# Thirty of 64 gathered rows fetched by TensorE instead of 28, with a uniform pairing of batches

## The chip, the cores and the metric

The kernel runs on one core of a Trainium2 chip. The metric is the device time of one execution in microseconds (us). Shares and rows are from one execution taken by the hardware profiler.

## The reference, cut to what matters

An image batch `x` (32 images, 64 channels, 16x16 pixels) goes through a group norm and a 3x3 convolution, a graph attention over 80,000 edges, and a mixture-of-experts block whose gate is a graph attention over 262,144 edges. The change touches only that last gate:

```
h = (x_flat @ W_gat).reshape(M, 4, 4)          # M = 8192 tokens
a_src = (h * att_src).sum(-1);  a_dst = (h * att_dst).sum(-1)
e     = leaky_relu(a_src[src] + a_dst[dst], 0.2)
ee    = exp(e - segment_max(e, dst)[dst]);  denom = segment_sum(ee, dst)
agg   = segment_sum(h[src] * (ee / denom[dst])[:, :, None], dst) + b_gat
```

So each edge needs the 16 numbers `h[src]` of its source node and the 4 numbers `a_src[src]`.

## The kernel before, in words

The edges lie sorted by destination, 128 partitions times 64 edges to a *chunk*. In this data 17 chunks hold edges (numbers 0 to 16). For chunks 0 and 1 GpSimd (POOL) fetches all 64 rows of `h` per partition from memory, one indirect DMA for each of the 64 columns (`g_gather`, L845). From chunk 2 on, 15 chunks in all, it fetches only 36 columns and the other 28 (`PICKS`, L65) are *picked* on chip: TensorE multiplies one-hot columns with `h_split`, a three-part bf16 copy of the table.

The 28 columns go in 7 batches of 4 (`BATCH`, `BATCHES`), and two batches share one set of one-hots (a *pair*, `w`; pair 3 has one batch and is 512 columns wide, the others 1024). The steps for chunk c are:

- `pick_keys` (L1965, VectorE): eight small operations turn the source numbers into keys; once for a chunk.
- `spread(m)` (L1061, TensorE): 4 matmuls lay the keys of batch m along the free axis of a PSUM bank.
- `all_keys(m)` (L1296, ScalarE): casts that bank into `pick_all`.
- `one_hot(w)` (L1990, VectorE): 8 comparisons (one for each of 8 table slices) write `pick_hot[w % 2]`.
- `pick(m)` (L1071, TensorE): 96 matmuls (4 columns x 8 slices x 3 parts) into one of two PSUM banks. It waits for the pair's one-hots and for batch m-2 to be taken (`pick_taken`).
- `take_picked(m)` (L1998, VectorE): a product from PSUM (L2002, recorded at L1391) and a reduce (L2006); the product's end releases `pick_taken`.
- `picked_a_src` (L2008, VectorE): `a_src` of the picked rows.

While chunk c is picked, the softmax work of chunk c-1, the chunk behind, is done between the takes: `flags`, then `edge_scores`, `maximum`, `messages`, `weighted_sums` on VectorE (L1922 to L1958), and `lay`, `weigh`, `rows` on ScalarE (L1259 to L1294). `lay` waits until all gathers of chunk c-1 have landed (L1270), and `edge_scores` waits for `lay`; `messages` waits for `weigh`; `rows` waits for `weighted_sums` (L1290) and copies the sums out. POOL may gather chunk c+1 once `messages` of chunk c-1 is done (`g_used`, L861). SyncE reloads index buffers after `lay` (L713).

Each engine runs its instructions in the order in which they stand in the code; nothing reorders them. The orders in the loop before are, for chunk c ((c+1) marks steps for the next chunk):

```
VectorE  flags | oh1 take0 edge_scores | take1 maximum | oh2 take2 messages |
         take3 weighted_sums | oh3 take4 | keys(c+1) take5 | oh0(c+1) take6 | a_src
TensorE  p0 s4 p1 s5 p2 s6 p3 p4 p5 s0(c+1) s1(c+1) p6 s2(c+1) s3(c+1)
ScalarE  lay k4 k5 weigh k6 rows k0(c+1) k1(c+1) k2(c+1) k3(c+1)
```

Here p is `pick`, s `spread`, k `all_keys`, oh `one_hot`.

Of the kernel before, what the change touches and what calls it, by code (L numbers as in the profile page):

```python
# [61 lines left out]
HID = 2 * CH  # L62


PICKS = 28  # L65
BATCH = 4
BATCHES = PICKS // BATCH
HOTS = -(-BATCHES // 2)
CANDS = 8
K_TILES = NT // CANDS  # L70
YT_FREE = 24
# [170 lines left out]
def build(nc, io, debug=None):  # L242
    with ExitStack() as ctx:
# [319 lines left out]
        def bc(ap, shape):  # L563
            return ap.to_broadcast(shape)

        def chunk_count(it, b, per, n):

            return it * (2 * per) + ((b - 2) * per + n)

        def turn_of(b, m):  # L570

            return (b * BATCHES + m) % 2

        def hot_of(w):

            return min(2, BATCHES - 2 * w) * BATCH * P


        @block.sync
# [291 lines left out]
        def _(pe):  # L871
# [189 lines left out]
            def spread(it, b, m):  # L1061

                if m == 0:
                    pe.wait_ge(pick_keys_set, it * 2 + (b - 1))
                pe.wait_ge(pick_all_set, chunk_count(it, b, BATCHES, m + 1))
                for k in range(BATCH):
                    last = nc.tensor.matmul(ps[turn_of(b, m)][:, k * P:(k + 1) * P], bc(pick_key[b][:, BATCH * m + k:BATCH * m + k + 1], [P, P]), ident16,  # L1067
                                            start=True, stop=True)
                last.then_inc(pick_spread, 1)

            def pick(it, b, m):  # L1071
                pe.wait_ge(pick_hot_set, chunk_count(it, b, HOTS, m // 2 + 3))
                pe.wait_ge(pick_taken, chunk_count(it, b, BATCHES, m + 1))
                for k in range(BATCH):
                    for t in range(K_TILES):
                        for n in range(SPLITS):
                            last = nc.tensor.matmul(ps[2 + turn_of(b, m)][:, k * PICK_W:(k + 1) * PICK_W], pick_hot[m // 2 % 2][t][:, (m % 2 * BATCH + k) * P:(m % 2 * BATCH + k + 1) * P],  # L1077
                                                    h_split[n][:, t * PICK_W:(t + 1) * PICK_W],
                                                    start=t == 0 and n == 0, stop=t == K_TILES - 1 and n == SPLITS - 1)
                last.then_inc(picked, 1)  # L1080
# [1 line left out]
            pe.wait_ge(h_split_set, 2)  # L1082
            pe.wait_ge(g_count_set, 1)

            pe.sem_inc(picked, 2)
            n_all = pe.value_load(g_count[0:1, 0:1], min_val=2, max_val=G_CHUNKS)
            with pe.If(n_all >= 3):
                for m in range(4):
# [1 line left out]
            with nc.Fori(1, G_CHUNKS // 2, engines=[mybir.EngineType.PE], hint_back_edge=True) as it:  # L1090
                for b in range(2):
                    with pe.If(it * 2 + b < n_all):
                        for m in range(BATCHES - 2):
                            pick(it, b, m)
                            if m + 4 < BATCHES:
                                spread(it, b, m + 4)
                        for m in range(2):
                            pick(it, b, BATCHES - 2 + m)
                            with pe.If(it * 2 + (b + 1) < n_all):
                                for k in range(2):  # L1100
                                    spread(it + b, 1 - b, 2 * m + k)


            pe.wait_ge(exp_taken, EXPERTS_EARLY)
# [56 lines left out]
        def _(act):  # L1161
# [59 lines left out]
            def weigh(c):  # L1221
                act.wait_ge(a_scored, c + 1)
                nc.scalar.activation(a_weight, a_score, ACT.Exp)
                nc.scalar.activation(a_msg[:, CH * A_RUN:], a_score, ACT.Exp).then_inc(a_weighed, 1)
# [71 lines left out]
            def all_keys(it, b, m):  # L1296
                act.wait_ge(pick_spread, chunk_count(it, b, BATCHES, m + 1))
                act.wait_ge(pick_hot_set, chunk_count(it, b, HOTS, m // 2 + 1))
                nc.scalar.copy(pick_all[m // 2 % 2][:, m % 2 * BATCH * P:(m % 2 + 1) * BATCH * P], ps[turn_of(b, m)][:, 0:BATCH * P]).then_inc(pick_all_set, 1)  # L1299

            def gelu(n):
                act.wait_ge(hid_done, n + 1)
# [17 lines left out]
            with act.Fori(1, G_CHUNKS // 2 + 1) as it:  # L1320
                for b in range(2):
                    with act.If(it * 2 + b < n_all):
                        lay(it, 1 - b, 1)
                        all_keys(it, b, 4)
                        all_keys(it, b, 5)
                        weigh(it, 1 - b, 1)
                        all_keys(it, b, 6)
                        rows(it, 1 - b, 1)
                        with act.If(it * 2 + (b + 1) < n_all):
                            for m in range(4):  # L1330
                                all_keys(it + b, 1 - b, m)
                    with act.If(it * 2 + b == n_all):
                        lay(it, 1 - b, 1)
                        weigh(it, 1 - b, 1)
                        rows(it, 1 - b, 1)
# [36 lines left out]
        def _(dve):  # L1372
# [17 lines left out]
            def tt(o, a_, b_, op):  # L1390
                return V.tensor_tensor(o, a_, b_, op)  # L1391
# [568 lines left out]
            def pick_link(it, b, ins):  # L1960
                p_done[0] += 1
                ins.then_inc(dve_pick, 1)
                dve.wait_ge(dve_pick, chunk_count(it, b, PICK_STEPS, p_done[0]))
# [25 lines left out]

            def one_hot(it, b, w):  # L1990

                dve.wait_ge(pick_all_set, chunk_count(it, b, BATCHES, min(2 * w + 2, BATCHES) + 2))
                dve.wait_ge(picked, chunk_count(it, b, BATCHES, (1, 2, 4, 6)[w]))
                for t in range(K_TILES):
                    ins = ts(pick_hot[w % 2][t][:, 0:hot_of(w)], pick_all[w % 2][:, 0:hot_of(w)], node[:, t:t + 1], ALU.is_equal)
                ins.then_inc(pick_hot_set, 1)

            def take_picked(it, b, m):  # L1998
                dve.wait_ge(picked, chunk_count(it, b, BATCHES, m + 3))
                at = slice(m * BATCH, (m + 1) * BATCH)  # L2000
                prod_ = pick_prod.rearrange("p (j k f) -> p j k f", k=CANDS, f=G_HF)
                pick_link(it, b, tt(prod_, ps[2 + turn_of(b, m)][:, 0:BATCH * PICK_W].rearrange("p (j k f) -> p j k f", k=CANDS, f=G_HF),  # L2002
                                    bc(pick_of[b].rearrange("p (j k) -> p j k", k=CANDS)[:, at, :, None], [P, BATCH, CANDS, G_HF]), ALU.mult))
                dve.sem_inc(pick_taken, 1)  # L2004
                lo = G_RUN - PICKS + m * BATCH
                pick_link(it, b, V.tensor_reduce(hs[b][:, lo:lo + BATCH, 0:G_HF], prod_.rearrange("p j k f -> p j f k"), AX_X, ALU.add))  # L2006

            def picked_a_src(it, b):  # L2008
                rows_ = hs[b][:, G_RUN - PICKS:]
# [19 lines left out]
            with nc.Fori(1, G_CHUNKS // 2 + 1, engines=[mybir.EngineType.DVE], head_slot={mybir.EngineType.DVE: 0}) as it:  # L2029
                for b in range(2):  # L2030
                    with dve.If(it * 2 + b < n_all):
                        p_done[0] = 0
                        flags(it, 1 - b, 1)
                        for m in range(BATCHES - 2):
                            if m % 2 == 0:
                                one_hot(it, b, m // 2 + 1)
                            take_picked(it, b, m)
                            if m < 4:
                                (edge_scores, maximum, messages, weighted_sums)[m](it, 1 - b, 1)
                        for m in range(2):  # L2040
                            dve.sem_inc(waits_carried, 1)
                            with dve.If(it * 2 + (b + 1) < n_all):
                                if m == 0:
                                    pick_keys(it + b, 1 - b)
                                    dve.sem_inc(waits_carried, 1)
                                else:
                                    one_hot(it + b, 1 - b, 0)
                            take_picked(it, b, BATCHES - 2 + m)
                        picked_a_src(it, b)
                        dve.sem_inc(waits_carried, 1)  # L2050
                        assert p_done[0] == PICK_STEPS
                    with dve.If(it * 2 + b == n_all):
                        flags(it, 1 - b, 1)
                        edge_scores(it, 1 - b, 1)
                        maximum(it, 1 - b, 1)
                        messages(it, 1 - b, 1)
                        weighted_sums(it, 1 - b, 1)
                        V.tensor_copy(row_tail, g_didx[1 - b][:, G_RUN - 1:G_RUN])
                        dve.sem_inc(waits_carried, 1)
# [178 lines left out]
```

## Time and profile before

| what | us |
|---|---|
| median of 3 runs (lowest, highest) | 2579.01 (2577.95, 2585.97) |
| the profiled execution's own time | 2578.7 |
| its span, first to last instruction | 2576.9 |
| busy: VectorE / GpSimd / TensorE matmul / ScalarE | 1802.0 / 1751.2 / 1149.8 / 681.6 |

```profile
## 2 busy tenths in 40 slices
PE   4552000001011000100105497789888898798286
DVE  8888679997879989884327301168768777778356
ACT  1110004434445343534201011222222222222121
POOL 0005777777777777777778577777777777777470
PEclk9775555555555555555555555589999999999558
```

Each digit is the busy share, in tenths, of one fortieth of the span, 64.4 us. The gate's chunk loop fills slices 27 to 37. A POOL that issues DMAs back to back reads 7, because the time between two issues is not counted as busy.

### The profile page before, as it was taken

What the parts mean: (1) busy time and instruction counts of PE and PEld (TensorE: products, weight loads), DVE (VectorE), ACT (ScalarE), POOL (GpSimd) and SP (SyncE); (2) the same over time, 40 slices, a digit from 0 to 9 for tenths busy, and PEclk for the clock granted to TensorE, in tenths of its full rate; (3) what the DMA queues carried; (4) which work ended last, traced back from release to release, by engine and by line L of the source; (5) the groups of instructions that cost most, each with busy time, mean ns of one, the idle gap of its engine ahead of it and who ended that gap; (6) DMA issues with size and microseconds to landing.
All of it is one profiled execution on the core that took longest, in us unless ns stands there. A gap on an engine that the chain in (4) does not pass through costs nothing.

```text
span 2576.9 us, 33597 instructions
## 1 busy us (share of the span) xinstructions
PE 1149.8 (45%) x12439; PEld 966.3 (37%) x12439; DVE 1802.0 (70%) x2767; ACT 681.6 (26%) x696; POOL 1751.2 (68%) x1690
## 2 busy tenths in 40 slices
PE   4552000001011000100105497789888898798286
PEld 2221000001000000000004254489888898798266
DVE  8888679997879989884327301168768777778356
ACT  1110004434445343534201011222222222222121
POOL 0005777777777777777778577777777777777470
PEclk9775555555555555555555555589999999999558
DMA  9402113333323333334314416122222222221101
GB/s 350 178 1 71 49 62 104 103 100 99 99 84 101 100 102 100 100 100 134 99 32 44 78 45 155 23 26 30 38 26 29 38 27 28 38 29 22 31 10 34
DMA packets 138177, 187.94 MB, mean 73 GB/s; under 512 B 77628, under 2 KB 96254, under 8 KB 131438
## 3 DMA queue, kind: packets, MB, share of 16 engines
q1 hardware_dynamic: 83958, 122.34, 14.6%
q0 software_dynamic: 54080, 63.61, 14.3%
q8 instruction: 105, 1.72, 0.3%
q14 instruction: 34, 0.28, 0.0%
HBM read 98.53 MB, written 87.32 MB: 72 GB/s over the span
## 4 chain that ended last, share of the span: by engine, by line
POOL 63%; issue 21%; DVE 10%; PE 3%; DMA 1%; ACT 1%; POOLq 0%; DVEq 0%; SPq 0%; ACTq 0%
POOL arena L751 59%; DVE arena L1391 8%; POOL d_adseed L841 2%; POOL d_qseed L775 2%; PE psum L1124 1%; PE psum L1155 1%; PE psum L1038 1%; DVE arena L1394 1%; DMA arena<-in_x 1%; PE psum L1050 1%; DMA arena<-d_gdst,arena 0%; PE psum L874 0%; ACT arena L1194 0%; DVE arena L1403 0%; PE psum L1116 0%
## 5 line engine op out<-in xcount | busy, mean ns | idle before, releaser
L1391 DVE TENSOR_TENSOR arena<-arena 128x512 f32<-128x512 f32 (+17 forms) x1331 | 766.3, 615 | 218.0 <-DMA arena<-d_ac,arena 65.7
L751 POOL DMA_INDIRECT arena<-d_h,arena x668 | 675.8, 1012 | 203.6 <-issue 203.6
L751 POOL DMA_INDIRECT arena<-in_kv,arena x640 | 662.3, 1035 | 195.0 <-issue 195.0
L1077 PE MATMUL psum<-arena 128*128 128x128 bf16 x10080 | 598.4, 222 | 45.1 <-DVEq L2004 29.8
L1077 PEld LDWEIGHTS psum<-arena 128*128 128x128 bf16 x10080 | 587.0, 99 | 50.1 <-DVE arena L1394 19.3
L874 PE MATMUL psum<-arena 128*128 128x128 f32 (+3 forms) x402 | 92.2, 399 | 1041.6 <-DVEq L1467 803.4
L874 PEld LDWEIGHTS psum<-arena 128*128 128x128 f32 (+3 forms) x402 | 70.5, 206 | 1064.3 <-DVEq L1467 818.5
L1391 DVE TENSOR_TENSOR arena<-psum,arena 128x512 f32<-128x512 f32 (+2 forms) x179 | 142.2, 802 | 231.3 <-PE psum L1038 202.6
L1394 DVE TENSOR_SCALAR arena<-arena 128x1024 bf16<-128x1024 f16 (+10 forms) x707 | 256.4, 414 | 35.1 <-DVE arena L2006 11.0
L751 POOL DMA_INDIRECT arena<-d_adst,arena x40 | 54.5, 1362 | 220.3 <-DVEq L1638 208.4
L1038 PEld LDWEIGHTS psum<-arena 128*128 128x128 f32 x512 | 113.7, 328 | 146.7 <-issue 110.4
L1038 PE MATMUL psum<-arena 128*128 128x64 f32 x512 | 125.1, 427 | 54.8 <-ACT arena L1305 38.5
L1792 DVE TENSOR_TENSOR_SCAN psum<-psum,arena 128x1024 f32<-128x1024 f32 x40 | 91.9, 2298 | 79.7 <-ACT arena L1218 78.5
L1050 PE MATMUL psum<-arena 64*128 64x512 f32 x128 | 131.5, 1135 | 0.6 <-ACT arena L1343 0.6
L1214 ACT COPY arena<-arena 128x1984 f32<-128x1984 f32 x20 | 73.1, 3655 | 214.6 <-DMA arena<-d_qseed 147.2
L1232 ACT COPY arena<-arena 128x2304 f32<-128x2304 f32 x20 | 87.8, 4391 | 155.5 <-DVEq L1814 155.5
L2006 DVE TENSOR_REDUCE arena<-arena 128x64 f32<-128x512 f32 x105 | 106.3, 1012 | 16.9 <-DVE arena L1391 11.5
L1305 ACT ACTIVATE arena<-psum,arena 128x512 f32<-128x512 f32 x64 | 43.7, 687 | 222.7 <-PE psum L1050 222.6
L1293 ACT COPY arena<-arena 128x1280 f32<-128x1280 f32 x17 | 57.3, 3373 | 158.7 <-DVEq L1957 158.7
L751 POOL DMA_INDIRECT arena<-d_gs,arena x64 | 67.2, 1050 | 42.6 <-SPq L734 23.4
L1391 DVE TENSOR_TENSOR arena<-arena,psum 128x2048 f32<-128x2048 f32 (+4 forms) x47 | 88.5, 1882 | 6.6 <-ACT psum L1285 2.3
L1299 ACT CAST arena<-psum 128x512 f16<-128x512 f32 x105 | 57.3, 587 | 133.4 <-PE psum L1067 133.4
(189 smaller groups left out, 1479.8 us busy)
## 6 DMA issues: line engine op xcount, KB each, us to landing
d_gs<-arena SPq DMA_DIRECT2D x32, 768.0 KB, 13.5
d_as<-arena SPq DMA_DIRECT2D x20, 1152.0 KB, 4.4
d_qseed<-arena SPq DMA_DIRECT2D x5, 4096.0 KB, 31.4
arena<-d_qseed SPq DMA_DIRECT2D x20, 1024.0 KB, 5.1
arena<-d_h,arena POOLq DMA_INDIRECT x668
arena<-in_kv,arena POOLq DMA_INDIRECT x640
d_adseed<-arena SPq DMA_DIRECT2D x1, 4096.0 KB, 29.2
arena<-in_w_blocks SPq DMA_DIRECT2D x1, 2304.0 KB, 20.2
```

The lines of the kernel that those rows point to most:

```text
L751: return pool.indirect_dma_start(out, None, table, bass.IndirectOffsetOnAxis(index[:, t:t + 1], 0))
L874: return nc.tensor.transpose(out, in_, ident[0:n, 0:n])
L1038: last = nc.tensor.matmul(ps[6 + k // 2][:, k % 2 * 256 + e * CH:k % 2 * 256 + (e + 1) * CH], hid[n % 2][:, k * P:(k + 1) * P], w2[:, e, : ...
L1050: nc.tensor.matmul(ps[4 + n % 2][:, :], w1[at, e, :], yT[at, i0:i0 + 4, :].rearrange("p i n -> p (i n)"), start=True, stop=True).then_inc( ...
L1077: last = nc.tensor.matmul(ps[2 + turn_of(b, m)][:, k * PICK_W:(k + 1) * PICK_W], pick_hot[m // 2 % 2][t][:, (m % 2 * BATCH + k) * P:(m % 2 ...
L1214: nc.scalar.copy(by_f[:, :, 1:], q_seed[b].rearrange("p j f -> p f j")[:, :, 1:])
L1232: nc.scalar.copy(a_rows[b].rearrange("p j f -> p f j"), a_sum.rearrange("p (f j) -> p f j", j=A_RUN)).then_inc(a_rows_set, 1)
L1293: nc.scalar.copy(rows_f[:, 0:G_F], g_sum.rearrange("p (f j) -> p f j", j=G_COLS)[:, :, 1:])
L1391: return V.tensor_tensor(o, a_, b_, op)
L1394: return V.tensor_scalar(o, a_, s1, s2, op0, op1) if op1 is not None else V.tensor_scalar(o, a_, s1, None, op0)
L1792: step(V.tensor_tensor_scan(q_edge, a_go, q_fm[:, at], 0.0, ALU.mult, ALU.add))
L2006: pick_link(it, b, V.tensor_reduce(hs[b][:, lo:lo + BATCH, 0:G_HF], prod_.rearrange("p j k f -> p j f k"), AX_X, ALU.add))
```

## The change

`PICKS` goes from 28 to 30, so POOL gathers 34 columns of each chunk from chunk 2 on. The batches become 8: seven of 4 columns and a last of 2. They form four pairs; the last pair is 768 columns wide. The waits are rewritten for this. Three orders change: the softmax work of the chunk behind starts after take1 instead of take0; the next keys are made before one-hot 3; the next chunk's first one-hots come after take5 and before take6 and take7.

```
VectorE  flags | oh1 take0 | take1 edge_scores | oh2 take2 maximum | take3 messages |
         keys(c+1) oh3 take4 weighted_sums | take5 | oh0(c+1) take6 take7 | a_src
TensorE  p0 s4 p1 s5 p2 s6 p3 s7 p4 p5 s0(c+1) s1(c+1) p6 s2(c+1) s3(c+1) p7
ScalarE  k4 lay k5 k6 weigh k7 rows k0(c+1) k1(c+1) k2(c+1) k3(c+1)
```

```diff
-PICKS = 28
+PICKS = 30
-BATCHES = PICKS // BATCH
-HOTS = -(-BATCHES // 2)
+BATCHES = -(-PICKS // BATCH)
+HOTS = BATCHES // 2
...
+        PICKED_FIRST = 4
+        def batch_of(m):
+            return min(BATCH, PICKS - m * BATCH)
         def hot_of(w):
-            return min(2, BATCHES - 2 * w) * BATCH * P
+            return (batch_of(2 * w) + batch_of(2 * w + 1)) * P
...
                         for m in range(2):
-                            pick(it, b, BATCHES - 2 + m)
                             with pe.If(it * 2 + (b + 1) < n_all):
                                 for k in range(2):
                                     spread(it + b, 1 - b, 2 * m + k)
+                            pick(it, b, BATCHES - 2 + m)
...
                     with act.If(it * 2 + b < n_all):
+                        all_keys(it, b, 4)
                         lay(it, 1 - b, 1)
-                        all_keys(it, b, 4)
                         all_keys(it, b, 5)
+                        all_keys(it, b, 6)
                         weigh(it, 1 - b, 1)
-                        all_keys(it, b, 6)
+                        all_keys(it, b, 7)
                         rows(it, 1 - b, 1)
                         with act.If(it * 2 + (b + 1) < n_all):
                             for m in range(4):
...
             def one_hot(it, b, w):
-                dve.wait_ge(pick_all_set, chunk_count(it, b, BATCHES, min(2 * w + 2, BATCHES) + 2))
-                dve.wait_ge(picked, chunk_count(it, b, BATCHES, (1, 2, 4, 6)[w]))
+                dve.wait_ge(pick_all_set, chunk_count(it, b, BATCHES, 2 * w + 4))
+                dve.wait_ge(picked, chunk_count(it, b, BATCHES, 2 * w + PICKED_FIRST - 2))
...
                         for m in range(BATCHES - 2):
+                            if m == 4:
+                                dve.sem_inc(waits_carried, 1)
+                                with dve.If(it * 2 + (b + 1) < n_all):
+                                    pick_keys(it + b, 1 - b)
+                                    dve.sem_inc(waits_carried, 1)
                             if m % 2 == 0:
                                 one_hot(it, b, m // 2 + 1)
                             take_picked(it, b, m)
-                            if m < 4:
-                                (edge_scores, maximum, messages, weighted_sums)[m](it, 1 - b, 1)
+                            if 1 <= m <= 4:
+                                (edge_scores, maximum, messages, weighted_sums)[m - 1](it, 1 - b, 1)
+                        dve.sem_inc(waits_carried, 1)
+                        with dve.If(it * 2 + (b + 1) < n_all):
+                            one_hot(it + b, 1 - b, 0)
                         for m in range(2):
-                            dve.sem_inc(waits_carried, 1)
-                            with dve.If(it * 2 + (b + 1) < n_all):
-                                if m == 0:
-                                    pick_keys(it + b, 1 - b)
-                                    dve.sem_inc(waits_carried, 1)
-                                else:
-                                    one_hot(it + b, 1 - b, 0)
                             take_picked(it, b, BATCHES - 2 + m)
                         picked_a_src(it, b)
```

`spread`, `pick`, `all_keys` and `take_picked` loop over `batch_of(m)` columns instead of `BATCH`. The first count given to `picked` goes from 2 to `PICKED_FIRST`.

## Rows read from the trace of the kernel before

**Rows 1.** The page: part 4 (chain by engine), part 5 (the gathers of `d_h`)
```profile
POOL 63%; issue 21%; DVE 10%; PE 3%; DMA 1%; ACT 1%; POOLq 0%; DVEq 0%; SPq 0%; ACTq 0%
...
L751 POOL DMA_INDIRECT arena<-d_h,arena x668 | 675.8, 1012 | 203.6 <-issue 203.6
```

**Rows 2.** Timeline (start us, us, engine, line, op), ScalarE: `lay`'s last copy
```profile
1788.22 0.20 ACT L1272 COPY arena<-arena 128x4 f32<-128x4 f32 x1 [5.62 <-DMA arena<-d_h,arena]
...
2407.93 0.20 ACT L1272 COPY arena<-arena 128x4 f32<-128x4 f32 x1 [11.27 <-DMA arena<-d_h,arena]
```

**Rows 3.** Timeline, VectorE, chunk 3: a chunk in which it hardly waits
```profile
1738.20 0.43 DVE L1391 TENSOR_TENSOR arena<-arena 128x256 f32<-128x256 int32 x1 [0.61 <-DVE arena L2012]
...
1742.09 0.68 DVE L1391 TENSOR_TENSOR arena<-psum,arena 128x512 f32<-128x512 f32 x1
...
1745.96 0.69 DVE L1391 TENSOR_TENSOR arena<-psum,arena 128x512 f32<-128x512 f32 x1
...
1747.85 0.70 DVE L1941 TENSOR_TENSOR_SCAN arena<-arena 128x260 f32<-128x260 f32 x1
...
1750.14 3.26 DVE L1394 TENSOR_SCALAR arena<-arena 128x1024 bf16<-128x1024 f16 x8 [0.31 <-DVE arena L1391]
...
1755.20 2.29 DVE L1391 TENSOR_TENSOR arena<-arena,psum 128x1024 f32<-128x1024 f32 x1
...
1759.54 2.87 DVE L1956 TENSOR_TENSOR_SCAN arena<-psum,arena 128x1300 f32<-128x1300 f32 x1
1762.70 2.54 DVE L1394 TENSOR_SCALAR arena<-arena 128x512 bf16<-128x512 f16 x8 [0.30 <-DVE arena L1956]
...
1767.41 0.42 DVE L1394 TENSOR_SCALAR arena<-arena 128x28 int32<-128x28 int32 x2 [0.42 <-DVE arena L2006]
...
1769.89 0.69 DVE L1391 TENSOR_TENSOR arena<-psum,arena 128x512 f32<-128x512 f32 x1
...
1772.16 3.49 DVE L1394 TENSOR_SCALAR arena<-arena 128x1024 bf16<-128x1024 f16 x8 [0.41 <-DVE arena L2006]
1775.57 0.68 DVE L1391 TENSOR_TENSOR arena<-psum,arena 128x512 f32<-128x512 f32 x1
1776.39 1.01 DVE L2006 TENSOR_REDUCE arena<-arena 128x64 f32<-128x512 f32 x1
1777.43 0.63 DVE L1391 TENSOR_TENSOR arena<-arena 128x448 f32<-128x448 f32 x1
...
1779.70 0.42 DVE L1391 TENSOR_TENSOR arena<-arena 128x256 f32<-128x256 int32 x1 [0.99 <-DVE arena L2012]
```

**Rows 4.** Timeline, ScalarE, chunk 3: `rows` (two copies), then two casts of `all_keys`
```profile
1762.49 3.38 ACT L1293 COPY arena<-arena 128x1280 f32<-128x1280 f32 x1 [9.86 <-DVEq L1957]
1765.60 0.92 ACT L1294 COPY arena<-arena 128x256 f32<-128x256 f32 x1
1769.12 1.07 ACT L1299 CAST arena<-psum 128x512 f16<-128x512 f32 x2 [2.60 <-PE psum L1067]
```

**Rows 5.** Timeline, TensorE: picks at full clock, with one `spread` between and without
```profile
1745.22 0.39 PE L1067 MATMUL psum<-arena 128*128 128x128 f16 x4
1745.44 5.52 PE L1077 MATMUL psum<-arena 128*128 128x128 bf16 x96
...
1751.03 16.24 PE L1077 MATMUL psum<-arena 128*128 128x128 bf16 x288
```

**Rows 6.** Timeline, TensorE: after a wait for `pick_keys`, at the lower clock
```profile
1908.55 1.03 PE L1067 MATMUL psum<-arena 128*128 128x128 f16 x8 [3.17 <-DVEq L1982]
1909.37 7.90 PE L1077 MATMUL psum<-arena 128*128 128x128 bf16 x96
```

**Rows 7.** Timeline, VectorE: take1 of chunk 2, then the softmax work of chunk 16
```profile
1705.00 0.69 DVE L1391 TENSOR_TENSOR arena<-psum,arena 128x512 f32<-128x512 f32 x1 [1.81 <-PE psum L1077]
...
2408.16 0.70 DVE L1932 TENSOR_TENSOR_SCAN arena<-arena 128x260 f32<-128x260 f32 x1 [13.61 <-ACT arena L1272]
...
2414.36 2.28 DVE L1391 TENSOR_TENSOR arena<-arena,psum 128x1024 f32<-128x1024 f32 x1 [2.31 <-ACT psum L1285]
```

More of the change, by code:

```diff
@@ L1065, in spread @@
                 pe.wait_ge(pick_all_set, chunk_count(it, b, BATCHES, m + 1))
-                for k in range(BATCH):
+                for k in range(batch_of(m)):
                     last = nc.tensor.matmul(ps[turn_of(b, m)][:, k * P:(k + 1) * P], bc(pick_key[b][:, BATCH * m + k:BATCH * m + k + 1], [P, P]), ident16,
@@ L1073, in pick @@
                 pe.wait_ge(pick_taken, chunk_count(it, b, BATCHES, m + 1))
-                for k in range(BATCH):
+                for k in range(batch_of(m)):
                     for t in range(K_TILES):
@@ L1083, in _ @@
             pe.wait_ge(g_count_set, 1)
-            pe.sem_inc(picked, 2)
+            pe.sem_inc(picked, PICKED_FIRST)
             n_all = pe.value_load(g_count[0:1, 0:1], min_val=2, max_val=G_CHUNKS)
@@ L1298, in all_keys @@
                 act.wait_ge(pick_hot_set, chunk_count(it, b, HOTS, m // 2 + 1))
-                nc.scalar.copy(pick_all[m // 2 % 2][:, m % 2 * BATCH * P:(m % 2 + 1) * BATCH * P], ps[turn_of(b, m)][:, 0:BATCH * P]).then_inc(pick_all_set, 1)
+                nc.scalar.copy(pick_all[m // 2 % 2][:, m % 2 * BATCH * P:(m % 2 * BATCH + batch_of(m)) * P], ps[turn_of(b, m)][:, 0:batch_of(m) * P]).then_inc(pick_all_set, 1)
             def gelu(n):
@@ L1998, in take_picked @@
             def take_picked(it, b, m):
[L1999 to L2003, printed above, removed]
+                dve.wait_ge(picked, chunk_count(it, b, BATCHES, m + 1 + PICKED_FIRST))
+                n_ = batch_of(m)
+                at = slice(m * BATCH, m * BATCH + n_)
+                prod_ = pick_prod[:, 0:n_ * PICK_W].rearrange("p (j k f) -> p j k f", k=CANDS, f=G_HF)
+                pick_link(it, b, tt(prod_, ps[2 + turn_of(b, m)][:, 0:n_ * PICK_W].rearrange("p (j k f) -> p j k f", k=CANDS, f=G_HF),
+                                    bc(pick_of[b].rearrange("p (j k) -> p j k", k=CANDS)[:, at, :, None], [P, n_, CANDS, G_HF]), ALU.mult))
                 dve.sem_inc(pick_taken, 1)
                 lo = G_RUN - PICKS + m * BATCH
-                pick_link(it, b, V.tensor_reduce(hs[b][:, lo:lo + BATCH, 0:G_HF], prod_.rearrange("p j k f -> p j f k"), AX_X, ALU.add))
+                pick_link(it, b, V.tensor_reduce(hs[b][:, lo:lo + n_, 0:G_HF], prod_.rearrange("p j k f -> p j f k"), AX_X, ALU.add))
             def picked_a_src(it, b):
```

## The prediction

> **What bounds the kernel now.** I read the chain of waits first, then the largest group on it, then one chunk on each engine. The chain lies on POOL for 63% of the span, and all idle time before the gathers of `d_h` is "issue": POOL never waits for another engine there [rows 1]. One gather costs (675.8 + 203.6) / 668 = 1.316 us, so 36 should take 47.4. The period shows it: `lay`'s last copy, which waits for the landing of a chunk's gathers, starts at 1788.22 for chunk 3 and at 2407.93 for chunk 16, 13 periods of 47.67 us [rows 2]. The reader is to see that ScalarE was idle there "until DMA". VectorE follows: in its pass for chunk 3, where it waits for almost nothing, it needs 1779.70 - 1738.20 = 41.5 us [rows 3]. At the end it waits 13.61 us for the last gathers, and from 2408.16 on the tail begins [rows 7]. The change doesn't touch the tail, so the question is only when that row starts.
>
> **What the change removes.** Two gathers in each of 15 chunks, 30 x 1.316 = 39.5 us of POOL. If POOL stayed the bound, the period would be 47.67 - 2.63 = 45.0 and the tail would start 39.5 us earlier, at 2368.7.
>
> **What it adds on VectorE.** Batch 7 has two columns. A full take is 1777.43 - 1775.57 = 1.86 us (product 0.68, reduce 1.01) [rows 3]; half the columns I put at 1.2 (bounds 0.9 and 1.86). One-hot 3 grows from 512 to 768 columns: before, it and take4 take 1767.41 - 0.42 - 1762.70 = 4.3, so one-hot 3 is 2.4; a full one is 3.3; between them 2.8. Together +1.6: 43.1 us of VectorE, under 45.0. The keys and `a_src` of 30 columns instead of 28 are below 0.1.
>
> **What it adds on TensorE.** A pick with one spread is 5.59 (1751.03 - 1745.44), a pick without one (16.24 - 5.52) / 2 = 5.36, so a column's picks are 1.34 and its spread 0.06 [rows 5]: 30 columns are 42 us at the full clock. That too is under 45.0.
>
> **What the new order does: the step that decides.** Sums of busy time are not the period. ScalarE's order is ... `rows`, then `all_keys` 0 and 1 of the next chunk. Before, `weighted_sums` followed take3; `rows` ran from 1762.49 to 1766.52 beside one-hot 3 and take4, and the casts came at 1769.12, after the keys [rows 4]. Now `weighted_sums` follows take4, and only take5 stands between it and the next one-hots, which need both casts. `rows` takes 4.03, the casts 1.07, with 0.1 at each end: 5.3 us from the end of `weighted_sums`. Take5 hides 1.9 of them; VectorE stands for 3.3. TensorE stands too: s2 waits for the first cast, and p7 is queued behind it. Making the keys early doesn't help, as the spreads they feed find ScalarE occupied.
>
> The longest loop through the engines, from the start of take1:
> - take1 1.89 (1747.85 - 1745.96); `edge_scores` 2.0 (1745.96 - 1742.09 - 1.86) and 0.2 before the next; one-hot 2 and take2 5.06 (1755.20 - 1750.14); `maximum` 2.29 - 0.31 = 1.98 [rows 3]. At 11.1. Pick 3 is ready then as well (two picks of 5.59 after pick 1).
> - `messages` needs `weigh`, 2.31 after `maximum` [rows 7]. Before, a one-hot and a take hid that; now take3 alone does, so 0.4 shows. At 13.4.
> - `messages` 2.45; keys 2.48 and some 0.3 before them; one-hot 3 2.8; take4 1.88; `weighted_sums` 2.87 [rows 3]. At 26.2.
> - `rows` and casts 5.3, at 31.5; one-hot 0 3.3 (3.49 busy, next op 3.41 later), at 34.8: take6 starts.
> - take6's product releases p0 0.9 later; p0 5.59, p1 5.56: take1 of the next chunk at 46.8. By VectorE alone (take6 1.86, take7 1.2, `a_src` and the gap 2.3, flags and one-hot 1 3.89, take0 1.86) it would be 45.9, so TensorE closes the loop.
>
> That is 46.8 at the full clock. On TensorE p6 ends at 27.9 and s2 comes at 30.9: a gap of 3.0 in each chunk, then two spreads half a microsecond apart, then p7. Before, eleven passes (chunks 5 to 15) had a wait of 3.2 for the keys. After four of them the spreads and pick 5 ran as in [rows 6], 1.03 and 7.90 against 0.6 and 5.52, a loss of 2.8; after two more the loss was 1.3; after five nothing. Here p7 ends 1.3 before p0 could start, so the long loss costs 1.5 and the short none: 4/11 x 1.5 = 0.55 a chunk. I take 47.4; bounds 46.8 (never) and 48.7 (every time, 1.9).
>
> The Trainium skill, page "TensorE: Matmul & The Clock Gate", section "HAM oscillation — how this bites in real kernels", says that a matmul loop with a wait in every pass can be thrown back to the low clock in every pass. By that rule the sum goes by the upper bound; the rows above agree only after some of the waits.
>
> **Waits and queues with no price.** `lay` moves behind `all_keys` 4, so it starts only after p0 and s4, about 2 us into the pass; `edge_scores` now comes after take1, 7 us in, and covers that. SyncE's index loads hang on `lay`; the next keys use them 15 us later. `all_keys` 5 is queued behind `lay`, so late gathers would hold s7 and one-hot 2; with VectorE behind POOL this doesn't bite. `messages` comes later, and POOL waits for it before chunk c+1; POOL has a whole chunk's gathers (45 us) to issue meanwhile, and by my period it runs ahead by 2.4 a chunk, some 34 us in all, about when that wait begins to hold it, harmlessly.
>
> **The sum.** Take1 of chunk 2 is at 1705.00 [rows 7], and all before it is unchanged. Its take6: 1739.8. Take6 of chunk 15: 13 periods on. The pass of chunk 16 has no keys and no next one-hots: take1 comes 12.0 after that, take6 waits for p6 at 12.0 + 27.9 = 39.9, take7 for p7 at 42.7; then take7 1.2, `a_src` and gap 2.3, flags 0.8: `edge_scores` of chunk 16 at 47.0. So it starts at 1786.8 + 13 x period. With 47.4 that is 2403.0, against 2408.16: 5.2 earlier. POOL is done by then (2368). The profiled execution took 2578.7 (1.8 of it around the span, 0.3 below the median of the runs); less 5.2 this gives 2573.5.
>
> **Forecast: 2573 us** (rounded down), 0.2% under the median, within the 0.3% (7.7 us) that a measurement can tell from no change. Its own range, from periods of 46.9 to 48.2, is 2567 to 2584. What is late next is ScalarE: VectorE's wait for gathers turns into a wait for its casts.
>
> **Rivals.**
> - *POOL stays the bound.* Then `rows` must not hold the casts, or VectorE must make up 2.4 a chunk elsewhere. For: 43.1 and 42 are both under 45.0. Against: ScalarE's queue order is in the code, and nothing in it overtakes. 2578.7 - 39.5 = 2539, or up to 2545 if the gathers that ran long beside one-hots stay as many. It would need a period under 44.8 by my formula. 13%.
> - *The clock never falls.* TensorE is busy for 42 of 47 us instead of 39 of 47.7, and has one gap of 3.0 instead of several. Period 46.8, start 2395.2, so 2565.7. 15%.
> - *The clock falls in every chunk: slower.* Place: the gap from p6 to s2, lengthened by two spreads that are hardly work. Price: 1.9 on p7 and p0, 48.7; start 2419.9, 11.7 later, 2590.4. It decides from a period of 47.8 on, where 1786.8 + 13 x period passes 2408. For: a gap that lies in front of near-idle time. Against: five of eleven such waits before cost nothing. 19%.
>
> The forecast has 53%: its spread crosses the lower bound, so 20 of the 53 count as faster, 30 as the same, 3 as slower. POOL and the full clock are faster (13, 15); the fallen clock gives 4 same and 15 slower. Faster 0.48, same 0.34, slower 0.18. The range reaches from 2550 to 2591; outside are POOL's 13% and about 6% above.
>
> **What would show it.** Right: the casts of `all_keys` 0 and 1 start directly behind `rows` with no idle time; one-hot 0 has about 3 us of idle time, released by ScalarE L1299; the spreads s2 wait for ScalarE; the flags-to-flags period is 47 to 48; POOL's last gathers of `d_h` have landed near 2368, long before the softmax work of chunk 16, which no longer waits for it. The first row in which `messages` waits for ScalarE L1285 has some 0.4 idle. Wrong: `lay` still waits for DMA at a period of 45, or POOL waits for VectorE from early on, or the wait for the casts is under 1 us.

## The result, and the profile after

The changed kernel takes 2570.12 us (median of 6 runs, 2565.67 to 2572.32) against 2578.48 for the kernel before (2577.45 to 2585.97): ratio 0.9961, 95% interval [0.9947, 0.9976]. Timed again in another job it was 2569.83 against 2576.92, ratio 0.9973 [0.9963, 0.9983]. The forecast was 2573 and an unmeasurable gain; the gain is small, 7 to 8 us, but it is clear of noise: both intervals end below 1. Most of the 39.5 us that POOL was relieved of did not arrive, as forecast.

The profiled execution took 2572.32, with a span of 2570.5. The page of the changed kernel, parts 4 and 5, and the loop's list of waits (engine, line, waited for: us, times, longest) answer to [rows 1]:

```profile
POOL 40%; DVE 23%; issue 17%; PE 15%; ACT 3%; DMA 1%; DVEq 1%; POOLq 0%; ACTq 0%; SPq 0%
...
L757 POOL DMA_INDIRECT arena<-d_h,arena x638 | 643.6, 1009 | 205.1 <-issue 196.3 <-DVEq L1960 8.2 <-DMA arena<-d_gdrow 0.6
```

```profile
DVE arena L1401 <- ACT arena L1305: 40.0, 13, 3.1
...
POOL arena L757 <- DVEq L1960: 8.2, 5, 2.7
```

POOL's share of the chain fell from 63% to 40%: in the chunk loop the chain now runs over VectorE, TensorE and ScalarE. POOL waits five times for `messages` (L1960), so it has run ahead as far as it may; its last gather of `d_h` begins at 2378.52, where the prediction had POOL done by 2368. VectorE waits 13 times between 1750 and 2390, up to 3.1 us, for a cast of `all_keys` (L1305).

VectorE, timeline of the changed kernel, from take1 to take1 of the next chunk, answers to [rows 3]:

```profile
2036.76 0.69 DVE L1398 TENSOR_TENSOR arena<-psum,arena 128x512 f32<-128x512 f32 x1 [1.08 <-PE psum L1083]
...
2045.78 0.70 DVE L1948 TENSOR_TENSOR_SCAN arena<-arena 128x260 f32<-128x260 f32 x1
...
2050.15 2.29 DVE L1398 TENSOR_TENSOR arena<-arena,psum 128x1024 f32<-128x1024 f32 x1 [0.36 <-ACT psum L1291]
...
2055.87 2.73 DVE L1401 TENSOR_SCALAR arena<-arena 128x768 bf16<-128x768 f16 x8 [0.30 <-DVE arena L1398]
...
2060.40 2.87 DVE L1963 TENSOR_TENSOR_SCAN arena<-psum,arena 128x1300 f32<-128x1300 f32 x1
...
2068.40 3.38 DVE L1401 TENSOR_SCALAR arena<-arena 128x1024 bf16<-128x1024 f16 x8 [3.13 <-ACT arena L1305]
2071.70 0.68 DVE L1398 TENSOR_TENSOR arena<-psum,arena 128x512 f32<-128x512 f32 x1
...
2077.18 0.49 DVE L1398 TENSOR_TENSOR arena<-arena 128x256 f32<-128x256 int32 x1 [0.97 <-DVE arena L2020]
...
2084.06 0.69 DVE L1398 TENSOR_TENSOR arena<-psum,arena 128x512 f32<-128x512 f32 x1 [1.13 <-PE psum L1083]
```

The same stretch on ScalarE answers to [rows 4]; the next fence, TensorE, to [rows 5, 6]:

```profile
2063.36 3.37 ACT L1299 COPY arena<-arena 128x1280 f32<-128x1280 f32 x1 [13.02 <-DVEq L1964]
2066.46 0.92 ACT L1300 COPY arena<-arena 128x256 f32<-128x256 f32 x1
2067.10 2.46 ACT L1305 CAST arena<-psum 128x512 f16<-128x512 f32 x4
```

```profile
2059.40 5.52 PE L1083 MATMUL psum<-arena 128*128 128x128 bf16 x96 [0.31 <-DVEq L2012]
2067.85 1.08 PE L1073 MATMUL psum<-arena 128*128 128x128 f16 x8 [2.94 <-ACT arena L1305]
2068.73 9.63 PE L1083 MATMUL psum<-arena 128*128 128x128 bf16 x144
2078.20 0.39 PE L1073 MATMUL psum<-arena 128*128 128x128 f16 x4
```

For comparison, a pass in which the clock held (TensorE, timeline):

```profile
1833.77 0.87 PE L1073 MATMUL psum<-arena 128*128 128x128 f16 x8 [2.94 <-ACT arena L1305]
1834.48 2.84 PE L1083 MATMUL psum<-arena 128*128 128x128 bf16 x48
1838.32 5.54 PE L1083 MATMUL psum<-arena 128*128 128x128 bf16 x96 [1.00 <-DVEq L2012]
```

The reader is to see three things. The casts start directly behind `rows`, with no idle time between. The spreads s2 and s3 then stand 2.94 us for the first cast and run slowly here: 1.08 for 8 matmuls, 0.87 where the clock held. Pick 7 and pick 0 (144 matmuls) take 9.63, where 5.52 + 2.68 = 8.2 would do. In ten of the 14 passes that have next keys to spread, the granted clock fell to its lower level (1.2 of 2.4 GHz) on the spreads or pick 7, and the two picks took 9.2 to 9.8. In the other four it held, and pick 0 then waited about 1 us for take6. So pick 7 has about 1 us to spare, and counted from s2 to the end of pick 0 a fallen clock cost 0 to 0.45 us (10.1 where it held, 10.1 to 10.5 where it fell).

The period, from flags to flags, is (2358.40 - 1748.19) / 13 = 46.94 us. The tail begins here, without a wait for gathers; this and chunk 16's flags answer to [rows 7] (VectorE, timeline):

```profile
2358.40 0.42 DVE L1398 TENSOR_TENSOR arena<-arena 128x256 f32<-128x256 int32 x1 [0.97 <-DVE arena L2020]
...
2401.30 0.70 DVE L1939 TENSOR_TENSOR_SCAN arena<-arena 128x260 f32<-128x260 f32 x1 [2.24 <-ACT arena L1278]
```

It starts 6.9 us earlier than 2408.16. The loop itself gained more: this execution came to take1 of chunk 2 at 1708.80, 3.8 later than before. The start of the gathers of `d_h`, ahead of all changed code, lies anywhere from 1522 to 1530 in the profiled executions of this study; it is 1525.9 in the one before and 1529.8 in this one, so these 3.8 us are the spread of single executions.

### The profile page after: what moved, and what is told of

Read it like the earlier page. It is cut to its first block, busy times and chain, and to the rows that moved or that the text cites. A ratio compares the mean times of both kernels' runs of the same rounds, so it can differ in the third digit from the quotient of the medians.

```text
span 2570.5 us, 35239 instructions
## 1 busy us (share of the span) xinstructions
PE 1186.7 (46%) x13189; PEld 1002.8 (39%) x13189; DVE 1825.8 (71%) x2797; ACT 683.8 (27%) x711; POOL 1721.3 (67%) x1660
## 4 chain that ended last, share of the span: by engine, by line
POOL 40%; DVE 23%; issue 17%; PE 15%; ACT 3%; DMA 1%; DVEq 1%; POOLq 0%; ACTq 0%; SPq 0%
POOL arena L757 36%; DVE arena L1398 12%; PE psum L1083 9%; DVE arena L1401 5%; POOL d_adseed L847 2%; DVE arena L1963 2%; PE psum L1044 2%; DVE arena L2014 2%; PE psum L1056 2%; POOL d_qseed L781 2%; PE psum L1130 1%; DMA arena<-in_x 1%; ACT psum L1291 1%; PE psum L1161 1%; ACT arena L1300 1%
## 5 line engine op out<-in xcount | busy, mean ns | idle before, releaser
L757 POOL DMA_INDIRECT arena<-d_h,arena x638 | 643.6, 1009 | 205.1 <-issue 196.3
L1083 PE MATMUL psum<-arena 128*128 128x128 bf16 x10800 | 633.7, 221 | 8.1 <-DVEq L2012 4.9
L1083 PEld LDWEIGHTS psum<-arena 128*128 128x128 bf16 x10800 | 622.7, 98 | 10.8 <-issue 5.8
L1398 DVE TENSOR_TENSOR arena<-psum,arena 128x512 f32<-128x512 f32 (+2 forms) x194 | 148.3, 772 | 237.6 <-PE psum L1044 202.5
L1401 DVE TENSOR_SCALAR arena<-arena 128x1024 bf16<-128x1024 f16 (+10 forms) x707 | 263.2, 424 | 71.5 <-ACT arena L1305 43.7
L2014 DVE TENSOR_REDUCE arena<-arena 128x64 f32<-128x512 f32 x120 | 116.1, 968 | 18.1 <-DVE arena L1398 11.3
L1311 ACT ACTIVATE arena<-psum,arena 128x512 f32<-128x512 f32 x64 | 43.7, 688 | 217.8 <-PE psum L1056 217.8
L1305 ACT CAST arena<-psum 128x512 f16<-128x512 f32 x120 | 65.7, 572 | 126.6 <-PE psum L1073 122.6
```

Source lines behind the costliest of these rows:

```text
L757: return pool.indirect_dma_start(out, None, table, bass.IndirectOffsetOnAxis(index[:, t:t + 1], 0))
L1401: return V.tensor_scalar(o, a_, s1, s2, op0, op1) if op1 is not None else V.tensor_scalar(o, a_, s1, None, op0)
L2014: pick_link(it, b, V.tensor_reduce(hs[b][:, lo:lo + n_, 0:G_HF], prod_.rearrange("p j k f -> p j f k"), AX_X, ALU.add))
```

## The experiments

My theory: what bounds the changed kernel is the place of `rows` in ScalarE's queue, in front of the two casts. The first rival is that 30 picks are simply 46.9 us of work for VectorE and TensorE; the others were POOL and the clock.

**Casts before `rows`.**

```diff
-                        rows(it, 1 - b, 1)
                         with act.If(it * 2 + (b + 1) < n_all):
-                            for m in range(4):
+                            for m in range(2):
                                 all_keys(it + b, 1 - b, m)
+                        rows(it, 1 - b, 1)
+                        with act.If(it * 2 + (b + 1) < n_all):
+                            for m in range(2, 4):
+                                all_keys(it + b, 1 - b, m)
```

> The changed kernel with one move on ScalarE: `all_keys` 0 and 1 of the next chunk before `rows`, 2 and 3 behind it. Theory (the queue): VectorE's 3.1 us wait for the casts goes, the loop through the engines is 26.2 + take5 2.2 + one-hot 3.3 + 12.0, about 44 us, which is under POOL's 45.0, so POOL becomes the bound: period 45.0 to 45.4, time 2539 to 2545. Rival (the work): 30 picks cost VectorE and TensorE so much that 46.9 is their own period; then the wait moves elsewhere and the time stays at 2565 to 2571.

Measured: 2540.74 us, ratio 0.9846 [0.9829, 0.9862]. VectorE's timeline shows one-hot 0 close behind take5 (1954.14, then 1956.41); from the pass of chunk 8 on ScalarE's `lay` waits for gathers again:

```profile
1956.41 3.26 DVE L1404 TENSOR_SCALAR arena<-arena 128x1024 bf16<-128x1024 f16 x8 [0.41 <-DVE arena L2017]
...
1965.06 0.43 DVE L1401 TENSOR_TENSOR arena<-arena 128x256 f32<-128x256 int32 x1 [0.97 <-DVE arena L2023]
```

```profile
2059.33 0.20 ACT L1278 COPY arena<-arena 128x4 f32<-128x4 f32 x1 [2.65 <-DMA arena<-d_h,arena]
```

The period is 44.0 while the engines set it (flags at 1745.28 and 1965.06, five passes) and 45.1 when POOL does (`lay`'s last copy at 1969.26 and 2375.07, nine passes). Both are the numbers worked out beforehand (44 and 45.0 to 45.4). VectorE no longer waits for a cast in any pass of this stretch. The change of order is worth 29 us; the same 30 picks are no obstacle. The rival of pure work falls.

**Four gathers less.** The edit sets `g_gather(b, G_RUN - PICKS - 4)` and the counts of `hs_in` to match.

> The changed kernel with 30 gathers in place of 34 in chunks 2 to 16 (four columns keep the rows of an earlier chunk, so part of the computation is left out). Theory: POOL is off the path, so nothing moves: 2568 to 2572, period 46.9, and POOL waits longer for `g_used`. Rival (POOL still sets part of the time, through late landings or by its DMAs getting in the way): 4 x 1.316 x 15 = 79 us less work on it takes 10 us or more off.

This leaves out part of the computation. Measured: 2568.61, ratio 0.9954 [0.9938, 0.9971]. That is 1.5 us under the changed kernel, within the noise, for 79 us less gathering. In the loop of this run, POOL's row by lines reads:

```profile
L757 POOL DMA_INDIRECT arena<-d_h,arena x446 | 452.9, 1015 | 220.5 <-issue 173.1 <-DVEq L1960 47.1 <-DMA arena<-d_gdrow 0.3
```

The wait for `messages` grew from 8.2 to 47.1 us, and the last gather began 6 us earlier (2372.39). POOL does not set the changed kernel's time.

**The chunk behind begins after take0, as before.**

```diff
-                            if 1 <= m <= 4:
-                                (edge_scores, maximum, messages, weighted_sums)[m - 1](it, 1 - b, 1)
+                            if m < 4:
+                                (edge_scores, maximum, messages, weighted_sums)[m](it, 1 - b, 1)
```

On ScalarE `lay` and `weigh` move forward with it; its order becomes lay k4 k5 weigh k6 k7 rows.

> The changed kernel with the chunk behind begun after take0 as before the change (and `lay` first on ScalarE, `weigh` after `all_keys` 5); the 30 picks, the early keys and the early one-hots stay. Theory: `weighted_sums` comes one batch earlier, so `rows` (4.0) and the two casts (1.1) lie beside keys, one-hot 3, take4 and take5 (8.8): no wait for casts, POOL bound, 2539 to 2545. Rival (the work): 2565 or more. If beginning later was needed for the landings of the gathers, VectorE waits for gathers in front of take1 and the time lies between, 2550 to 2560.

Measured: 2544.84, ratio 0.986 [0.9843, 0.9876]. The casts stay behind `rows` here, and yet VectorE's wait for them is gone: `weighted_sums` comes a batch earlier. This is a second way to remove the same wait. So "one batch later" is what put `rows` in the way. With the early keys and the early one-hots still in place the time is within the noise of the first experiment's (the intervals overlap), so these two cost nothing that shows.

**A longer `rows`.** One more copy of 128x256 into a spare tile, ahead of `rows`' last copy.

> The changed kernel with one more copy of 128x256 on ScalarE in `rows`, into a spare tile: 0.6 to 0.9 us for each chunk between `weighted_sums` and the casts. Theory: ScalarE lies on the loop there, so each chunk is longer by that: 14 x 0.6 to 0.9, 8 to 13 us more than the changed kernel, 2578 to 2583. Rival (the work, or POOL): ScalarE is busy for 27% of the span and has room; 2570 as before.

Measured: 2579.4, ratio 0.9997 [0.9987, 1.0007], 9.3 above the changed kernel. The copies of `rows` now hold the casts 0.45 us longer (4.18 us from the first copy to the casts, 3.73 in the changed kernel), and VectorE's wait in front of one-hot 0 grew from 3.0 - 3.1 to 3.5 - 3.6:

```profile
2067.51 3.44 DVE L1403 TENSOR_SCALAR arena<-arena 128x1024 bf16<-128x1024 f16 x8 [3.56 <-ACT arena L1307]
```

The period is (2360.18 - 1790.81) / 12 = 47.45, 0.5 more. An engine that is busy for 27% of the span sets the period here, about one for one. The medians differ by somewhat more than 13 such periods (9.3 against 6.6 us); I have not followed the rest.

**Pick 7 before s2.** TensorE's order becomes s0 s1 p6 p7 s2 s3.

> The changed kernel with TensorE's order s0 s1 p6 p7 s2 s3 instead of s0 s1 p6 s2 s3 p7: pick 7 no longer stands behind the spreads that wait for ScalarE. Theory: pick 7 has 1.3 us to spare and isn't on the loop; what closes it is take6 releasing pick 0. The period stays 46.9, time 2566 to 2572, and TensorE's gap moves between p7 and s2. Rival (TensorE's stall in front of p7 is what costs): 1 us or more a chunk less, 2556 or below. Rival (the clock): pick 0 now starts directly behind the gap at the lower clock, and up to 1.5 a chunk is lost, 2580 to 2590.

Measured: 2588.68, ratio 1.0041 [1.0025, 1.0056], 18.9 above the changed kernel in the same job (2569.83). My theory's number (2566 to 2572) was wrong, that of the rival, the clock (2580 to 2590), right. TensorE:

```profile
2028.86 0.88 PE L1073 MATMUL psum<-arena 128*128 128x128 f16 x8 [0.26 <-ACT arena L1308]
2033.29 6.80 PE L1083 MATMUL psum<-arena 128*128 128x128 bf16 x96 [3.55 <-DVEq L2015]
```

and VectorE's take1 behind it:

```profile
2045.79 0.69 DVE L1401 TENSOR_TENSOR arena<-psum,arena 128x512 f32<-128x512 f32 x1 [2.44 <-PE psum L1083]
```

Pick 0 now runs directly behind the gap, 6.80 in place of 5.52; take1 waits 2.44 in place of 1.1. The period is (2375.71 - 1749.55) / 13 = 48.17, 1.23 more. Pick 0 ran slowly in all 14 passes (6.77 to 8.40). In the changed kernel the low clock falls mostly on pick 7, which has about 1 us to spare.

**The new order with 28 picks.** The kernel before, with the three moves of the change and nothing else.

> The kernel before (28 picks, 36 gathers) with the new order alone: chunk behind one batch later, keys before one-hot 3, ScalarE's order to match (k4 lay k5 k6 weigh rows). Theory: `rows` then holds the casts here too, the loop is 46.8 less 0.4 for the narrow one-hot, 46.4, still under POOL's 47.67, so the wait is paid out of VectorE's slack and the time is that of before, 2576 to 2582. Its trace should have about 3 us of VectorE idle time for each chunk released by the casts. Rival (the new order slows by itself): 2585 or more. Rival (it speeds up by itself): under 2570.

Measured: 2580.69, ratio 1.0013 [1.0004, 1.0022]. The time lies in the expected range, the mechanism doesn't: the period is (2369.93 - 1747.48) / 13 = 47.88, not 46.4, so the order alone makes the engines slower than POOL. TensorE shows why:

```profile
2074.94 0.88 PE L1067 MATMUL psum<-arena 128*128 128x128 f16 x8 [2.81 <-ACT arena L1299]
2079.07 7.69 PE L1077 MATMUL psum<-arena 128*128 128x128 bf16 x96 [3.26 <-DVE arena L1394]
```

With 28 picks no pick 7 stands behind s3, so two gaps, 2.81 and 3.26, follow each other with two spreads between, and pick 0 takes 7.69, 2.2 more than at the full clock. It took 7.6 to 8.2 in all 14 passes. Of this, the period shows 1.5 us against the 46.4 worked out beforehand.

**The same with the casts before `rows`.** The edit is that of the first experiment.

> The kernel with 28 picks and the new order (the run before it of this kind had a period of 48.0, above POOL's 47.67), with `all_keys` 0 and 1 of the next chunk cast before `rows`. Theory: the wait for the casts and the low clock behind it go, VectorE's own loop falls to about 42.5, POOL bounds again at 47.67, 2574 to 2579, and `lay` waits for gathers in each chunk. Rival (the new order costs something besides the casts): it stays at 2580 to 2583 with a period of 48.

Measured: 2572.3, ratio 0.9979 [0.9969, 0.9989]; 1.7 under the lower end expected. From the pass of chunk 6 on `lay` waits for gathers again (ScalarE):

```profile
2171.39 0.20 ACT L1272 COPY arena<-arena 128x4 f32<-128x4 f32 x1 [7.95 <-DMA arena<-d_h,arena]
```

With POOL as the bound, the order costs nothing that shows except through the casts. The expectation that the low clock would go with the wait was wrong: pick 0 still stands 2.0 to 3.8 us for its one-hots and took 7.0 to 8.3 in 12 of 14 passes, and before POOL set the pace the period was (1921.28 - 1743.83) / 4 = 44.4, not 42.5. It lies hidden under POOL's. Why this kernel is 5 us under the kernel before, at the same number of gathers, I haven't tested; its profiled execution, 2578.67, was the slowest of its nine and can't show it.

**32 picks.** The first experiment's order, `PICKS = 32`.

> The next step on ScalarE's corrected order: casts of `all_keys` 0 and 1 before `rows`, and 32 picks with 32 gathers (four full pairs). POOL's period would be 32 x 1.316 and some stalls, 42.4 to 43. Theory: the loop through VectorE and TensorE is 44.0 plus 0.5 (one-hot 3) and some 0.2 for the full batch 7, and TensorE alone needs 32 x 1.4 = 44.8, so the period is 44.8 to 45.3, the same as POOL's at 30 picks: 2537 to 2546. Rival (POOL is all that bounds): 2501 to 2510. Rival (TensorE's falling clock): over 2550.

Measured: 2551.39, ratio 0.9903 [0.9887, 0.9918]. The period, (2334.99 - 1836.99) / 11 = 45.27, is as expected, the time 5 us above. TensorE is now busy for 594.4 of the 600 us from 1750 to 2350 (572.5 with 30 picks), so it is the next limit. For the 5 us I have an argument and no test: I had forgotten the end. With POOL no longer last, the final pass runs at the engines' pace (43.7 from flags to flags) and there is no wait for gathers left to absorb it.

**31 picks.** Last batch of 3, last pair 896 wide.

> 31 picks (last batch of 3, last pair 896 columns) and 33 gathers, with the casts before `rows`. By the rows of the runs with 30 and 32 picks: the loop was 44.0 at 30 and 45.2 at 32, TensorE 31 x 1.4 = 43.4, so 44.4 to 44.8; the tail starts 13 x 0.6 later than the loop of the 30-pick run would let it, but that one waited 10 us for POOL's last gathers, which now land 20 us earlier. Time 2533 to 2540, a little under the 30-pick version. Rival (a loop at TensorE's limit of 45.2 as with 32 picks): 2545 to 2550.

Measured: 2536.62, ratio 0.9836 [0.9819, 0.9852], the fastest. Its period is (2322.25 - 1744.89) / 13 = 44.41. The intervals of 30 and 31 picks overlap; both beat the changed kernel by some 30 us.

**The changed kernel again.**

> The changed kernel once more, for a narrower interval in the same job. Expected ratio 0.996 to 0.998 of before. The formula 1786.8 + 13 x 46.9 for the start of the tail gives 11.7 less than before.

Measured as given above: 0.9973. From 1750 to 2350 us of the span, the views by window (us, busy of each engine, granted clock in the last column but two) read, for the changed kernel, pick 7 moved, casts first with 30, and the kernel before:

```profile
1750.00:2350.00 600.00, 556.77 (x9608) 550.19 (x9606) 486.56 (x880) 158.75 (x246) 453.15 (x447) 0.97 0.22 31
```

```profile
1750.00:2350.00 600.00, 552.06 (x9403) 544.34 (x9401) 474.41 (x861) 153.34 (x241) 444.28 (x436) 0.96 0.21 30
```

```profile
1750.00:2350.00 600.00, 572.50 (x10181) 568.53 (x10179) 513.89 (x930) 163.76 (x255) 462.79 (x451) 1.00 0.23 32
```

```profile
1750.00:2350.00 600.00, 523.05 (x8856) 516.20 (x8854) 463.46 (x851) 154.45 (x228) 462.25 (x453) 0.96 0.23 32
```

With 30 picks and the casts first the clock stays at its full level (1.00) in this stretch. Between the first two the mean hardly differs, 0.97 and 0.96; it fell in ten passes and in all 14, and what differs most is which pick is struck. The kernel before has 0.96 as well.

## Why the prediction was right

**The deciding step** held: the period comes from the queue of ScalarE and not from sums of busy time. Its terms, measured from take1 at 2036.76:

| point | predicted | measured |
|---|---|---|
| `messages` starts | 13.4 | 13.39 |
| `weighted_sums` ends | 26.2 | 26.51 |
| one-hot 0 starts | 31.5 | 31.64 |
| take6 starts | 34.8 | 34.94 |
| take1 of the next chunk | 46.8, 47.4 with the clock | 47.30; 46.94 over 13 passes |

Wait for the casts: 3.3 predicted, 3.0 to 3.1 found. Wait of `messages` for `weigh`: 0.4, found 0.36. Take7 1.2: found 0.42 and 0.59 with a gap of 0.15. One-hot 3 2.8: 2.73. POOL runs ahead and is held a little at the end, as said. Two of the signs named beforehand missed narrowly: the period is 46.94 and not 47 to 48, and POOL's last gather begins at 2378.52 and not near 2368, since POOL started 3.9 us later and was held for 8.2.

**The clock term** was mis-sized. I took 0.55 a chunk from [rows 6], four long losses in eleven; the period shows 0.14. Both factors were off, and in opposite directions. The clock fell in ten of 14 passes and not in four of eleven, and such a fall cost 0 to 0.45 us and not 1.5. That the product came near is in part luck. The count of four in eleven, and of five waits that "cost nothing", looked only at the spreads and pick 5 right behind the wait. In three of those five passes of the kernel before pick 6 was slow instead, behind a second gap:

```profile
1957.20 5.52 PE L1077 MATMUL psum<-arena 128*128 128x128 bf16 x96
1962.56 0.61 PE L1067 MATMUL psum<-arena 128*128 128x128 f16 x8
1965.30 7.16 PE L1077 MATMUL psum<-arena 128*128 128x128 bf16 x96 [2.13 <-DVEq L2004]
```

So the clock fell in nine of these eleven passes. The rival, "the clock falls in every chunk, 1.9 each", was nearer in how often. It was wrong in price, since pick 7 and the 1 us behind it took the loss. The two experiments with nothing to spare there, pick 7 moved and 28 picks, have periods 1.2 and 1.5 us longer than without the fall (the second against the 46.4 worked out): the rival's mechanism is real and its place was off by one pick. The Trainium skill, page "TensorE: Matmul & The Clock Gate", section "HAM oscillation — how this bites in real kernels", says that a matmul loop with a wait in every pass can be thrown back to the low clock in every pass. Those two runs agree, with pick 0 at 6.80 and 7.69 against 5.52 in the rows shown and slow in all 14 passes of each; the changed kernel agrees in ten passes of 14.

**The sum.** 13 periods at 46.94 instead of 47.4 give 6.0 us more gain. The last pass took 2401.30 - 2352.91 = 48.4 from take6 instead of 47.0: `lay` starts only when flags are set, and loads a table first, so VectorE waited 2.24. Together 4.6 more than the forecast's 5.2, 9.8; less the 3.8 by which this execution was late, 6.0; the rows say 6.9 and the run 6.4. The medians say 7 to 8. The longer last pass (1.4 against) and the shorter period (6.0 for) partly cancel, which also helps the forecast.

**The rivals.** "POOL stays the bound" would have been 2539; it takes one move on ScalarE to make it true, and that run came to 2540.74. "The clock never falls", 2565.7, is 4 us from the result and nearer on the period (46.8 against 46.94) than my 47.4, but not about the clock.

## What to carry to other kernels

Before moving a step later on one engine, read what that step releases on the others and what is queued behind it there: a copy of 4 us on an engine busy for a quarter of the time cost 29 us, because the casts that fed the bottleneck stood behind it. Once an engine's relief uncovers a loop, add the loop's terms along its waits; sums of busy time (43 and 42 against POOL's 45) promised 39 us that the order didn't allow. And an engine's spare time has a place: a gap of 3 us on TensorE was nearly free in front of a pick with 1 us to spare, and gaps of 3 to 4 us cost 1.2 and 1.5 us a pass in front of one with none.

## What the runs showed of the hardware

Two waits of 2.8 and 3.3 us with only eight small matmuls between them slow TensorE more reliably than one wait of 3.2 did before. With 28 picks and the new order, pick 0 took 7.6 to 8.2 in all 14 passes, where 5.52 is the full clock. In the kernel before, the pick right behind the one wait ran at full speed in five passes of eleven; but in three of these five the next pick, behind a second gap of 2.1 to 2.3 us, took 7.0 to 7.2. Short gaps can be enough: with 28 picks and the casts first, pick 0 took 7.16 behind a gap of 2.05 us (at 2105.72), and the pick ahead of it 7.15 behind one of 2.48. And a single gap is no sure sign: in the changed kernel the same 2.9 us in front of s2 went with a fallen clock in ten passes and with the full clock in four. What decides between the two no run here tests.
